# One attention-plus-experts block on one core: VectorE's chains of small steps split into half steps between row maxima

## The reference

```python
mod = (_silu(L0_c) @ L0_wmod).reshape(L0_c.shape[0], 6, 1, -1)
sa, ca, ga, sb, cb, gb = (mod[:, i] for i in range(6))      # ga, gb then kept at least 0.25 from zero
h = _layernorm(x) * (1 + ca) + sa
x = x + ga * attention(h)            # softmax(Q K^T / 4 + causal) V, then W_o and b_o
h = _layernorm(x) * (1 + cb) + sb
logits = h @ gate_w                  # 8 experts; the two largest, softmax over the two
x = x + gb * sum_over_top2(weight * silu(h @ w1[e]) @ w2[e])
```

## Time and profile before

| quantity | us |
|---|---|
| median of three runs | 1213.97 |
| the profiled execution | 1219.14 |
| its span, first to last instruction | 1217.1 |
| busy: TensorE | 959.1 |
| busy: VectorE | 736.8 |
| busy: ScalarE | 575.2 |
| busy: GpSimd | 351.6 |

### The profile page before, as it was taken

How to read it: one execution, slowest core, us unless ns; L and a number is a source line. 1 busy time by engine, 2 the same in 40 slices (tenths; PEclk the granted TensorE clock), 3 DMA queues, 4 the chain that set the end, 5 groups by cost and what they waited for, 6 DMA issues and landing times.

```text
span 1217.1 us, 19713 instructions
## 1 busy us (share of the span) xinstructions
PE 959.1 (79%) x6198; PEld 563.8 (46%) x6272; DVE 736.8 (61%) x2302; ACT 575.2 (47%) x1247; POOL 351.6 (29%) x303
## 2 busy tenths in 40 slices
PE   6778898988998888988896862084399996999980
PEld 3334433334343344343243430021398995898970
DVE  6668666786568875758764680032636444345885
ACT  3334655654856675756573620077233542333420
POOL 1430031233231234311333317602321305003566
PEclk8898899999999999989998876598699998899995
DMA  7437647452353264055255412224022223225775
GB/s 256 111 78 177 141 165 155 65 116 47 38 117 60 58 127 69 6 120 76 71 103 83 155 30 103 87 70 127 9 88 89 77 71 109 74 74 158 224 219 166
DMA packets 102101, 126.86 MB, mean 104 GB/s; under 512 B 17706, under 2 KB 75746, under 8 KB 102002
## 3 DMA queue, kind: packets, MB, share of 16 engines
q1 hardware_dynamic: 95042, 107.51, 36.7%
q0 software_dynamic: 6144, 16.79, 4.4%
q10 hardware_dynamic: 816, 1.32, 0.3%
HBM read 70.30 MB, written 50.74 MB: 99 GB/s over the span
## 4 chain that ended last, share of the span: by engine, by line
PE 55%; DVE 16%; issue 9%; ACT 6%; DMA 6%; SPq 3%; another core or an unknown queue 3%; POOL 2%; POOLq 0%; DVEq 0%; ACTq 0%
PE PH L1242 9%; PE PY L1242 9%; PE PO L1361 7%; PE PS L1341 7%; PE PM L1318 6%; DVE JK L1067 4%; PE PHT L1436 3%; ACT PR L893 2%; PE PX L1373 2%; DMA QK<-CD 2%; DVE MXF L1070 2%; SPq L601 2%; PE PX L1287 2%; PE PX L1296 1%
## 5 line engine op out<-in xcount | busy, mean ns | idle before, releaser
L893 ACT ACTIVATE PR<-PS 128x512 f32<-128x512 f32 (+3 forms) x768 | 333.8, 497 | 259.9 <-PE PS L1345 171.2
L1341 PE MATMUL PS<-QK 128*128 128x512 bf16 (+3 forms) x739 | 243.9, 341 | 79.3 <-ACT PR L893 33.7
L1318 PE MATMUL PM<-QK 128*128 128x512 bf16 (+3 forms) x723 | 242.9, 343 | 62.6 <-DVE MXF L1070 33.5
L1067 DVE CUSTOM_DVE_ANT_0 JK<-PM,MK 128x128 bf16<-128x128 f32 (+3 forms) x512 | 238.6, 484 | 83.1 <-PE PM L1318 64.8
L1070 DVE TENSOR_REDUCE MXF<-PM 128x1 f32<-128x512 f32 x256 | 175.6, 686 | 159.1 <-PE PM L1318 85.5
L1341 PEld LDWEIGHTS PS<-QK 128*128 128x128 bf16 x768 | 76.9, 101 | 252.5 <-ACT PR L893 133.3
L1361 PE MATMUL PO<-PR,V 128*17 128x512 f32 (+3 forms) x1536 | 170.6, 518 | 2.1 <-DVE MXA L1067 0.5
L1318 PEld LDWEIGHTS PM<-QK 128*128 128x128 bf16 x768 | 77.5, 101 | 147.6 <-DVE MXF L1070 60.0
L1242 PE MATMUL PH<-W1H,XT 128*128 x312 | 103.8, 415 | 45.3 <-DVE XT L1198 32.2
L952 ACT ACTIVATE HS<-PH 128x512 f32<-128x512 f32 x78 | 46.7, 598 | 183.2 <-PE PH L1242 136.8
L1345 PE MATMUL PS<-MT,identb 128*128 128x128 bf16 x512 | 114.4, 227 | 3.8 <-DMA QK<-CD 1.7
(11 more groups left out here) (206 smaller groups left out, 1381.1 us busy)
## 6 DMA issues: line engine op xcount, KB each, us to landing
QK<-SD SPq DMA_DIRECT2D x180, 128.0 KB
SD<-SP SPq DMA_DIRECT2D x42, 256.0 KB, 3.0
XL<-XS SPq DMA_DIRECT2D x78, 128.0 KB
YS<-YO SPq DMA_DIRECT2D x78, 128.0 KB
XS<-TM SPq DMA_DIRECT2D x12, 768.0 KB, 7.9
OP<-OS SPq DMA_DIRECT2D x64, 64.0 KB
LP<-LR SPq DMA_DIRECT2D x64, 64.0 KB, 2.3
W1L<-in_w SPq DMA_DIRECT2D x4, 1024.0 KB, 13.9
```

The costliest lines, as they stand in the source:

```text
L893: eng.activation(PR[:, slot, i, c0:512], PS[m % 3][:, c0:512], ACT.Exp, scale=0.25).then_inc(S["exp"].sem, 1)
L1067: eng.tensor_tensor_reduce(JK[:, jk % 2, 0:w], PM[m % 3][:, 0:w], MK[:, 512 - w:512], 1.0, -3.0e38, ALU.add, ALU.max, MXA[:, mb, h, qt:qt ...
L1318: eng.matmul(PM[m % 3][:, 0:128 * (k1 - k0)], QK[:, r, h, 0, qt * 128:(qt + 1) * 128], QK[:, r, h, 1, k0 * 128:k1 * 128], start=True, stop ...
L1341: last = eng.matmul(PS[m % 3][:, c0:512], QK[:, r, h, 1, j * 128:(j + 1) * 128], QK[:, r, h, 0, 512 * f + c0:512 * f + 512], start=True, s ...
```

## The change

`LEAD` goes from 31 to 34, so maxima, `cmax` and `crow` are further ahead of their scores. A second list of due steps at half slots is served between the first maximum and the second score of each slot. `cmax` becomes six steps and `rstd` sixteen, each one instruction, half a slot apart; the first batch's two (before the attention starts) and the chain of group 0 keep no delay. Where `ln2` runs in bursts of four (`pace` 4: batch 2 in window 13, batch 3 in the feed-forward stretch) the sixteen come in four bursts. `crow` follows the last step of `cmax` by 1.5 slots (`CROW`): in all, `cmax` starts at slot -10 and `crow` is at -6. The residual store is the first part of `ln2`. The MAX8 and search of `route`'s parts 0 and 1 become steps `top`, two tiles each, behind the logits that they read; logits of batches 0 and 1 move five slots later. `route` starts with its part 2, for batches 0 to 2 at slot 21 of window 13 (before: part 0 at 20).

```diff
-LEAD = 31
+LEAD = 34
+CROW = 1.5
 def stats(b):
-            + [(1, ("rstd", 1, b, n, 2)) for n in range(3)])
+            + [(0.5, ("rstd", 1, b, n, 2)) for n in range(16)])
...
-def ln2(b, wait=3, pace=1):
-    parts, d = [], 0
+def ln2(b, wait=3, pace=1, rest=0.5):
+    parts, d = [(0, ("x2", b))], 0
...
-    parts += [(d, ("rstd", 2, b, 0, 2)), (1, ("rstd", 2, b, 1, 2)), (1, ("rstd", 2, b, 2, 2)), (0, ("x2", b))]
+    parts += [(d if n == 0 else rest if n % pace == 0 else 0, ("rstd", 2, b, n, 2)) for n in range(16)]
...
-def logits(b, tp):
-    return [(0, ("lgt", b, tp)), (1, ("lg", b, tp))]
+def logits(b, tp, rest=0.5):
+    return [(0, ("lgt", b, tp)), (1, ("lg", b, tp)), (rest, ("top", b, tp, 0)), (rest, ("top", b, tp, 1))]
-def route(s):
-    return [(min(n, 1), ("route", s, n)) for n in range(8)]
+def route(s, rest=1):
+    return [(rest if n > 2 else 0, ("route", s, n)) for n in range(2, 8)]
...
-            place(4 * b + 8, 4 + 2 * tp, logits(b, tp))
+            place(4 * b + 8, 9 + 2 * tp, logits(b, tp))
-    place(NG - 3, 20, route(0))
+    place(NG - 3, 21, route(0))
...
-            place(g, n // 2 - LEAD, [(0, ("cmax", g, f)), (3 if g else 2, ("crow", g, f))])
+            place(g, n // 2 - LEAD, [(0.5 if g and i else 0, ("cmax", g, f, i)) for i in range(f == 0, 6)]
+                  + [(CROW if g else 2, ("crow", g, f))])
...
-        now[0] = t
+        now[0] = t - 0.5
...
             order.append(fill[0])
+        while at.get(now[0]):
+            run(at[now[0]].pop(0))
+        at.pop(now[0], None)
+        now[0] = t
         if score:
             order.append(("score", *score, 1))
         order += fill[1:]
...
-    place(13, ln2(B - 1, 1, 4))
+    place(13, ln2(B - 1, 1, 4, 1))
-        place(21 + 2 * tp, logits(B - 1, tp))
+        place(21 + 2 * tp, logits(B - 1, tp, 0))
```

In the engines' programs the instructions are the same. VectorE's `rstd` and `cmax` issue the one instruction of their step after a wait for the step before; ScalarE's `norm` and `h2` wait for step 15 and TensorE's `crow` for step 5 of their chains; `top` waits for its logits and for the `top` before it:

```diff
+                elif kind == "top":
+                    b, tp, part = a
+                    dv.wait_ge(*after("lg", "lg", b, tp))
+                    dv.wait_ge(S["top"], S["top"].before[step])
+                    for n in range(b * NT + 2 * tp, b * NT + 2 * tp + 2):
+                        if part == 0:
+                            eng.max(V8[:, n, :], LG[:, n, :]).then_inc(S["top"].sem, 1)
+                        else:
+                            eng.max_index(I8[:, n, :], V8[:, n, :], LG[:, n, :]).then_inc(S["top"].sem, 1)
```

More of the change, by code:

```diff
@@ L95, in stats @@
         return ([(min(n, 1), ("stat", b, n)) for n in range(NT)]
-                + [(1, ("rstd", 1, b, n, 2)) for n in range(3)])
+                + [(0.5, ("rstd", 1, b, n, 2)) for n in range(16)])
     def stats0(half):
         return ([(0, ("stat", 0, 4 * half + n)) for n in range(4)]
-                + [(0, ("rstd", 1, 0, n, half)) for n in range(3)])
-    def ln2(b, wait=3, pace=1):
-        parts, d = [], 0
+                + [(0, ("rstd", 1, 0, n, half)) for n in range(16)])
+    def ln2(b, wait=3, pace=1, rest=0.5):
+        parts, d = [(0, ("x2", b))], 0
         for n in range(NT):
@@ L289 @@
     "max": {"m": 1, "mx": 1},
-    "cmax": {"cp": lambda g, f: 5 + (f > 0)},
+    "cmax": {"cp": 1},
     "crow": {"px": 1, "ct": 1, "cd": 16, "crow_a": lambda g, f: 16 * (f == 0), "crow": lambda g, f: 16 * (f > 0)},
@@ L850, in scalar_program @@
                     b, half = a
-                    ac.wait_ge(*after("rstd", "rstd", 1, b, 2, 2 if b else half))
+                    ac.wait_ge(*after("rstd", "rstd", 1, b, 15, 2 if b else half))
                     xn_free(ac, step)
@@ L916, in scalar_program @@
                     b, tp = a
-                    ac.wait_ge(*after("rstd", "rstd", 2, b, 2, 2))
+                    ac.wait_ge(*after("rstd", "rstd", 2, b, 15, 2))
                     ac.wait_ge(S[f"x2{b}"], 16)
@@ L1071, in vector_program @@
                 elif kind == "cmax":
[L1072 removed]
+                    g, f, n = a
                     q0, q1 = 4 * (f == 1), 8 - 4 * (f == 0)
[L1074 removed]
+                    top, cp = MXA[:, g % 2, :, q0:q1], S["cp"]
                     part, rest = CP if f == 2 else CPH[:, f], CR[:, :, q0:q1]
                     dv.wait_ge(*after("mx", "max", g, (NM if f else NM0) - 1))
[L1077 removed]
+                    dv.wait_ge(cp, cp.before[step])
+                    if n == 0:
                         eng.tensor_tensor(MXA[:, g % 2, :, 4:8], MXA[:, g % 2, :, 4:8], MXF[:, g % 2, :, :], ALU.max).then_inc(cp.sem, 1)
[L1079 to L1090 removed]
+                    elif n == 1:
+                        if g > 1:
+                            dv.wait_ge(*after("px", "crow", g - 1, 2))
+                        eng.tensor_tensor(part[:, 0, :, :], top, top, ALU.max).then_inc(cp.sem, 1)
+                    elif n == 2:
+                        eng.tensor_tensor(rest, top, part[:, 0, :, :], ALU.subtract).then_inc(cp.sem, 1)
+                    elif n == 3:
+                        eng.tensor_tensor(part[:, 1, :, :], rest, rest, ALU.max).then_inc(cp.sem, 1)
+                    elif n == 4:
+                        eng.tensor_tensor(rest, rest, part[:, 1, :, :], ALU.subtract).then_inc(cp.sem, 1)
+                    else:
+                        eng.tensor_tensor(part[:, 2, :, :], rest, rest, ALU.max).then_inc(cp.sem, 1)
                 elif kind == "crow":
@@ L1116, in vector_program @@
                     dv.wait_ge(rt, c)
-                    if part == 0:
-                        dv.wait_ge(*after("lg", "lg", SEGS[s][1] - 1, 3))
-                        for n in range(n0, n0 + nt):
-                            eng.max(V8[:, n, :], LG[:, n, :]).then_inc(rt.sem, 1)
-                    elif part == 1:
-                        for n in range(n0, n0 + nt):
-                            eng.max_index(I8[:, n, :], V8[:, n, :], LG[:, n, :]).then_inc(rt.sem, 1)
-                    elif part == 2:
+                    if part == 2:
+                        dv.wait_ge(*after("top", "top", SEGS[s][1] - 1, 3, 1))
                         eng.tensor_copy(IF[:, sl, :], I8[:, sl, 0:2]).then_inc(rt.sem, 1)
@@ L1323, in tensor_program @@
                     px_free(pe, step)
-                    pe.wait_ge(*after("cp", "cmax", g, f))
+                    pe.wait_ge(*after("cp", "cmax", g, f, 5))
                     eng.transpose(PX[:, :].bitcast(BF16)[0:n, 0:128], cp.rearrange("p s h q -> p (s h q)") if f < 2 else
```

51 lines of the change are left out of this document (16 added, 35 removed).

## The result

The changed kernel takes 1161.0 us (median of four runs, 1158.75 to 1163.81) beside 1213.6 us for the kernel before (four runs, 1212.38 to 1217.64): a ratio of 0.956, 95% interval 0.953 to 0.959. The gain is 52.6 us where 31.6 were forecast.

The account below looks back on a forecast made before the run. TensorE's idle time in the attention stretch was taken to bound the gain, some 60 us. Terms summed to 35.6 us, less 4 for VectorE's backlog: 31.6 us, so 1182 us from a median of 1213.97; range 1165 to 1206.

Parts of the forecast that it names:

- Part 2, the clock: Attention stretch: TensorE work at the lower clock behind five QK<-CD waits speeds up, 6 us (0 to 9).
- Part 1, the waits of the lead: Attention: earlier maxima shorten eight QK<-CD waits, 11.6 us net (7 to 17); three output-projection waits go, 3.1 us.
- The price: Odd windows: `crow`'s transpose waits for ScalarE's q/k copy to free PSUM bank PX, 0.85 us six times, 5.1 us.
- The prologue: Before the first score: eight slots of maxima instead of five, costing 2.0 us.
- Part 3, the square roots: Reciprocal square roots spread one per half slot: two thirds of fourteen TensorE waits go, 7.9 us (3 to 11.9).
- Part 4, `cmax`: Six-step chain that splits the maxima, spread over slots 14 to 16.5: half its TensorE waits go, 5.6 us.
- The rival of the blocking: GpSimd blocks the spread `cmax` steps; TensorE waits about 42 us instead of 11.2, total 1223 us; chance 0.08.
- Part 5, the routing: Slots 20 and 21: clumped maxima and searches become pieces of two beside the logits, 2.4 us (1 to 2.8).
- Part 6, the store: Store of X2 moved to the front of `ln2`: zero, or 2 to 3 us lost without cover for the loads.
- The deduction of 4 us: Without the eight QK<-CD waits VectorE's backlog is partly met at the next maxima, half a microsecond each (0 to 10).
- The signs to look for: QK<-CD waits at most 0.5 us, no .50 at group starts, new L883 wait near 0.85 us, among others.
- The rival that came nearest: Nearly all TensorE waits go and the clock stays up: 46.5 us gained, 1167 us; chance 0.12.

Follow-up runs that it names:

- lead alone: Kernel before with maxima three slots further ahead and `crow` four slots behind `cmax`, chains in their old clumps: 1099.16 us beside 1142.52, ratio 0.965.
- and square roots: Kernel before with maxima three slots further ahead and square roots split; `cmax` whole, routing clumped, store behind the square roots: 1167.53 us, ratio 0.960.
- work in place of the wait: Kernel before with eight useless TensorE matmuls ahead of the QK<-CD wait in six windows: 1210.14 us beside 1213.12, ratio 0.997.
- the routing in clumps: Changed kernel with routing maxima and searches in two clumps at slots 20 and 21 of window 13: 1090.23 us beside 1142.52, ratio 0.957.

## Why the prediction was right in direction and too small

The lengths of the stretches of four kernels, from the rows above and the same view of the two kernels between (us):

| stretch | before | lead alone | and square roots | after |
|---|---|---|---|---|
| group 0 to 1 | 76.75 | 70.67 | 68.50 | 67.13 |
| group 1 to 2 | 43.32 | 40.32 | 41.18 | 40.29 |
| group 2 to 13 | 479.73 | 445.43 | 435.42 | 435.74 |
| group 13 to 14 | 60.24 | 60.72 | 63.31 | 57.34 |
| sum | 660.04 | 617.14 | 608.41 | 600.50 |

So the lead is worth 43 us, the square roots 9, the rest 8, each in the trace. Whole times give nearly the same: 43.4 for the lead, 9.2 for the square roots (by clumping them again), 6.5 for the rest. They come from different sets of runs and sum to 59.1, where the whole change gave 52.6 in one set and 56.8 in another, so a few of these microseconds are noise.

The forecast was 25.6 us of waits and 6 of clock; over the four stretches the traces show 35.5 and 24.1.

- **Part 2, the clock, is the term that failed: 6 us forecast (0 to 9), 18.0 measured in the long stretch alone.** Its mechanism was right, its size was not. The prediction counted the 0.50 stretches behind five waits for QK<-CD, and not five others, of the same length in all, near waits for VectorE's chains, the exponentials and the projection, though one of them follows a wait that it lists (2.18 us at 211.20). All ten hold 37.7 us of TensorE work; half of that is 18.9, and 18.0 came. The second omission is before 134 us, where the prediction prices no clock: between group 0 and 1 there were 15.4 us less of 0.50 and 5.0 us less busy time. The Trainium skill (TensorE: Matmul & The Clock Gate, "HAM oscillation — how this bites in real kernels") tells of a kernel that loses the clock at every DMA wait between its blocks of matmuls; the traces agree in part: the ten stretches stand near waits of 1.03 to 3.2 us, of which only half are for a DMA, and waits of 2.32 and 2.77 us had no 0.50 behind them.
- **Part 1, the waits of the lead, was right.** QK<-CD fell by 16.7 us (16.7 forecast), the projection's wait by 3.1 (3.1). The price was right in its mechanism and size: from 134 us to group 14's scores the transpose waited for L883 six times, 0.87 us each and 5.2 in all (0.85 and 5.1 forecast; the difference as printed there is 0.83). Not foreseen: two waits of 1.4 us for `cmax`'s last step. The prologue cost 1.0 us (2.0 forecast: the first score starts at 55.88 and not at 54.88).
- **Part 3, the square roots, was right:** 7.9 us forecast (3 to 11.9), 9 measured, clock included. VectorE's busy time in the long stretch is 4.1 us less than with the clumps (334.83 to 330.72, 1170 records each), though the instructions' own lengths sum to the same within 0.4 us: they overlap more. That bears on the rule on chained instructions that the prediction weighed (Trainium skill, VectorE: DVE Perf Modes, "Rules for kernel authors"): by it VectorE would have saved nothing.
- **Part 4, `cmax`, failed in its mechanism:** 5.6 us forecast for the splitting, none measured. The part had the sentence that spreading the chain over slots 14 to 16.5 doesn't remove its meetings with GpSimd. Going to slot 14 removed more than half of what they cost (34.9 us of steps down to 24.4 with the chain whole), and the splitting brought it back (36.3) and gained nothing. That TensorE's waits for banks fell by 5.3 us with the lead alone, near the 5.6, is luck.
- **The rival of the blocking** had its mechanism right. In window 6 of after the chain's last step, on VectorE, and GpSimd's multiplication:

```profile
349.52 1.85 DVE L1093 TENSOR_TENSOR CP<-CR 128x32 bf16<-128x32 f32 x1
...
348.98 2.35 POOL L781 TENSOR_TENSOR OP<-OP,LP 128x1024 f32<-128x1024 f32 x1 [24.89 <-DMA LP<-LR]
```

  The step ends at 351.37, GpSimd at 351.33, and the transpose L1331 started at 351.52 after 1.45 us of waiting. The Trainium skill's rule (SBUF — State Buffer, "Who interferes with whom") says so much: two SBUF inputs on VectorE exclude a reading GpSimd for a whole instruction; the trace agrees. What was off is the price on TensorE: its waits for banks were 8.0 us in the long stretch, not the 42 that this rival needed. (Seven times 4.7 and six times 3.6, at 2.2 for 2.5, is 48 and not 42; the rival would stand at 1229.) That three PSUM banks cover a single blocked step would explain it; no run tried another number of banks.
- **Part 5, the routing:** 2.4 us forecast, 6 to 7 measured in window 13 by clumping it again. Against the kernel before the window gained only 2.9, since with the lead, the square roots split and the routing clumped it had become 3.1 us longer (60.2 to 63.3). Part 6, the store, was put at zero, and nothing speaks against it; by itself it was not tried.
- **The deduction of 4 us** for VectorE's backlog didn't show: its banks' waits fell by 5.3 us in all with the lead alone, though those behind diagonal maxima rose from 10.8 to 13.3.
- The signs to look for held: one wait for QK<-CD, of 0.5 us; no 0.50 at the group starts; 0.87 us at L1331 in odd windows; no wait over 1 us behind the square roots or the searches; waits for banks from 134 to 677 us, the stretch that answers to the earlier trace rows, 15.2 us in place of 39.4. One sign looked at the wrong steps: the three that were to be longer if it went badly are shorter (676, 185 and 169 ns for L1084, L1088 and L1078), and two others, L1093 and L1085, are blocked in their place (679 and 478 ns), without harm.

The rival that came nearest, nearly all waits gone and the clock up (1167, at 0.12), was right that the clock stays up; its 9 us for that were still too little. It took 10 us for `cmax`, whose splitting gave nothing, and 15.2 us of waits for banks stayed.

Open: why one wait has the low clock behind it and another of its length has not, and how much of the 10 to 18 us that go with the clock would be left if something else ended next; the run with work in place of the wait shows 8.7 us in its stretch and 3 in the whole.

## What to carry to other kernels

Before pricing a wait on a TensorE-bound stretch, list every stretch of low granted clock and the wait ahead of each: here such stretches gave back 18.0 us beside 26.0 of idle time, and not only behind the wait that the change was aimed at. Which waits have one behind them differs from run to run, so take it as a range. Starting the round trip and its chain earlier was worth 43 us here where the wait for the round trip was 17: other waits fell with it, and the low clock went. Splitting paid for the square roots, and not for the chain whose single steps another engine blocks; these are two cases and no rule.

## What the runs showed of the hardware that was not expected

Chips differ by 6% on this kernel (1213 to 1218 us on two, 1142.5 on a third), and most of the difference has a place. From group 14's first score to the end of the attention, with GpSimd's 48 scatters in it, the kernel after in the run of the result:

```profile
656.38:777.08 120.70, 57.78 (x376) 18.21 (x380) 25.81 (x92) 42.70 (x100) 46.92 (x48) 0.70 0.32 100
...
PE PS L1347 <- issue: 38.5, 5, 26.7
```

and the kernel with the routing in clumps on the third chip:

```profile
664.48:727.04 62.56, 52.05 (x386) 17.32 (x383) 24.95 (x90) 41.70 (x98) 40.61 (x42) 0.93 0.54 173
```

That is 58 us of difference; behind the end of the attention another 19 (379.8 and 360.5 us to the end of the span), which no run explains. In the first, TensorE stands for up to 26.7 us at a score with nothing in the profile to wait for, while GpSimd issues, and VectorE and ScalarE stand as well; on the third chip it works on beside the same scatters. The prediction gave this block zero because the change doesn't shorten it, which held (121.6 us before, 120.7 after); what holds the engines there in one case and not in the other stays open.
